# VectorE's chain of slot tables and gather rows in five parts behind five successive shared tiles

## The reference

```
x = x + attention(layernorm(x), ctx, ctx, masks)
xf = layernorm(x)
ys = geglu(xf @ Ws1 + bs1) @ Ws2 + bs2            # shared expert, 512 hidden
logits = (xf @ Wr + br) / 1.5                     # 12 experts
top_val, top_idx = top_k(logits, 2);  w = softmax(top_val)
yE[e] = geglu(xf @ We1[e] + be1[e]) @ We2[e] + be2[e]   # 768 hidden
x = x + ys + sum over the two chosen experts of w * yE
```

## Time and profile before

| | us |
|---|---|
| median of 3 runs | 753.22 |
| lowest, highest | 750.91, 760.72 |
| profiled execution, its own time | 759.51 |
| its span in the profile | 757.7 |
| PE busy in it | 646.5 (85%) |
| VectorE busy | 484.7 (64%) |
| POOL busy | 347.5 (46%) |
| ScalarE busy | 300.7 (40%) |

### The profile page before, as it was taken

The page is one execution under the profiler, slowest core; times in us unless marked ns, Lnnn a source line. Parts: engine busy times, 40 slices in busy tenths (PEclk is TensorE's granted clock), DMA queues, the critical chain, the costliest instruction groups (busy, mean ns, idle before and its releaser), DMA issues.

```text
span 757.7 us, 14868 instructions
## 1 busy us (share of the span) xinstructions
PE 646.5 (85%) x4276; PEld 536.5 (71%) x4277; DVE 484.7 (64%) x1077; ACT 300.7 (40%) x685; POOL 347.5 (46%) x404
## 2 busy tenths in 40 slices
PE   7889989998968287699999999999999999993264
PEld 6778777877755265587878878787887878883163
DVE  7667767768734237976666767676666666762086
ACT  4445555554532042135434444444444444430021
POOL 3950000000120707796497489478974860027500
PEclk9989999999965668999999999999999999996687
DMA  9964522536010300553443544353545320113311
GB/s 294 402 218 163 210 107 101 208 140 251 24 47 1 117 8 17 177 181 114 153 166 119 193 148 167 123 193 133 194 129 177 121 78 28 35 42 119 90 42 56
DMA packets 48178, 100.07 MB, mean 132 GB/s; under 512 B 4624, under 2 KB 23824, under 8 KB 48144
## 3 DMA queue, kind: packets, MB, share of 16 engines
q1 hardware_dynamic: 36320, 51.06, 19.0%
q0 software_dynamic: 11120, 48.24, 19.0%
q10 hardware_dynamic: 704, 0.33, 0.2%
HBM read 58.19 MB, written 39.19 MB: 129 GB/s over the span
## 4 chain that ended last, share of the span: by engine, by line
PE 72%; DVE 10%; issue 7%; another core or an unknown queue 5%; ACT 5%; POOL 1%; DMA 1%; DVEq 0%; ACTq 0%; SPq 0%; POOLq 0%
PE ps_s L657 27%; PE ps_o L704 8%; PE ps_o L708 5%; PE ps_t L557 4%; PE ps_o L569 4%; PE ps_s L545 4%; PE ps_t L671 3%; PE ps_t L484 2%; ACT probT L832 2%; PE ps_x L484 2%; PE ps_s L540 2%; DVE x_all L1403 2%; PE ps_x L679 1%; PE ps_s L671 1%
## 5 line engine op out<-in xcount | busy, mean ns | idle before, releaser
L657 PE MATMUL ps_s<-ring,xTh 128*128 (+1 forms) x644 | 193.0, 422 | 13.2 <-issue 12.6
L657 PEld LDWEIGHTS ps_s<-ring,xTh 128*128 128x128 f32 x644 | 112.1, 192 | 31.4 <-issue 13.5
L1313 DVE TENSOR_TENSOR ag<-ps_s,up_bias 128x512 f32<-128x512 f32 x145 | 99.9, 689 | 26.3 <-remote 14.4
L657 PE MATMUL ps_s<-ring,xTl 128*128 (+1 forms) x322 | 101.6, 397 | 0.0
L1437 POOL TENSOR_TENSOR ring<-stage,ring 128x512 fp32r<-128x512 f32 x80 | 100.6, 1291 | 1.2
L1425 POOL TENSOR_TENSOR ve<-mv,eps 128x2 f32<-128x2 f32 x16 | 3.9, 247 | 207.2 <-DVE mv L1122 166.0
L704 PE MATMUL ps_o<-ring,hTh 128*128 x258 | 95.9, 409 | 1.0 <-DVE hTl L1322 1.0
L708 PE MATMUL ps_o<-ring,hTl 128*128 (+1 forms) x322 | 92.5, 287 | 0.0
L906 ACT ACTIVATE hTh<-ps_t 128x256 fp32r<-128x256 f32 x118 | 45.2, 384 | 109.8 <-PE ps_t L671 80.1
L899 ACT ACTIVATE ps_s<-ag 128x256 f32<-128x256 f32 x161 | 62.6, 389 | 48.8 <-DVE ag L1313 45.2
L1318 DVE TENSOR_TENSOR ag<-ag,ps_s 128x256 f32<-128x256 f32 x161 | 67.7, 421 | 20.2 <-ACT ps_s L899 2.1
(11 more groups left out here) (253 smaller groups left out, 1275.1 us busy)
## 6 DMA issues: line engine op xcount, KB each, us to landing
rows_in<-y_row SPq DMA_DIRECT2D x8, 3328.0 KB, 11.2
stage<-in_w POOLq DMA_DIRECT2D x12, 1536.0 KB, 6.7
stage<-in_w POOLq DMA_DIRECT2D x12, 768.0 KB
up_bias<-in_bias POOLq DMA_DIRECT2D x12, 768.0 KB, 4.6
xrow<-rows_in SPq DMA_DIRECT2D x43, 128.0 KB, 2.3
rows_out<-y_row SPq DMA_DIRECT2D x43, 128.0 KB, 1.7
cbuf<-in_ctx SPq DMA_DIRECT2D x8, 256.0 KB, 3.2
xn_all<-xn2p SPq DMA_DIRECT2D x8, 256.0 KB
```

The lines of the kernel that those rows point to most:

```text
L657: last = pe_.matmul(ps_s[:, i, :], x[:, c, :], weights(place, off + c * full + i * 2 * D, 2 * D), start=n == 0, stop=n == 5)
L1313: vec.tensor_tensor(ag[i][:, :, :].rearrange("p a n -> p (a n)"), ps_s[:, i, :], bias, ALU.add)\
```

## The change

The two functions of the chain are cut into five pieces: slot_experts, slot_places, slot_rows, out_rows_base with out_rows(0), and out_rows(1). The first stays behind tile 3, the others stand behind tiles 4, 5, 6 and 7. The two operations that write tab_ring and tab_need move into the second piece. The loop over tiles 4 to 7 on VectorE is written out. No other engine's stream changes; the waits of SyncE, POOL and PE are where they were.

```diff
--- before.py
+++ after.py
@@ -1239,22 +1239,23 @@
             def over_tiles(a):
                 return a.rearrange("p (o e) -> p o e", o=1).broadcast_to(wide)
 
-            def out_rows():
-
-                shape = [P, TILES, E]
+            def out_rows_base():
+
                 chain(vec.tensor_tensor(base_e[:, :], cum_e[:, :], tiles_e[:, :], ALU.subtract))
                 chain(vec.scalar_tensor_tensor(base_e[:, :], base_e[:, :], float(P), const[:, C_REGION:C_REGION + E],
                                                ALU.mult, ALU.subtract))
                 chain(vec.tensor_tensor(pos[:, :, :], pos[:, :, :],
-                                        base_e[:, :].rearrange("p (o e) -> p o e", o=1).broadcast_to(shape), ALU.add))
-                for k, pick in enumerate((pick1, pick2)):
-                    chain(vec.tensor_tensor(eq[:, :, :], pos[:, :, :], pick[:, :, :], ALU.mult))
-                    chain(vec.tensor_reduce(best[:, :], eq[:, :, :], AX.X, ALU.add))
-                    last = vec.tensor_copy(idx_out[:, k, :], best[:, :])
-                    if k == 0:
-                        chain(last)
-                    else:
-                        last.then_inc(out_rows_ready, 1)
+                                        base_e[:, :].rearrange("p (o e) -> p o e", o=1).broadcast_to([P, TILES, E]), ALU.add))
+
+            def out_rows(k):
+
+                chain(vec.tensor_tensor(eq[:, :, :], pos[:, :, :], (pick1, pick2)[k][:, :, :], ALU.mult))
+                chain(vec.tensor_reduce(best[:, :], eq[:, :, :], AX.X, ALU.add))
+                last = vec.tensor_copy(idx_out[:, k, :], best[:, :])
+                if k == 0:
+                    chain(last)
+                else:
+                    last.then_inc(out_rows_ready, 1)
 
             def first_rows():
 
@@ -1268,15 +1269,23 @@
                 chain(vec.tensor_scalar(tiles_e[:, :], cnt_s[:, :], 1.0, None, ALU.max))
                 chain(vec.tensor_tensor_scan(cum_e[:, :], ones_e[:, :], tiles_e[:, :], 0.0, ALU.mult, ALU.add))
 
-            def tile_tables():
+            def slot_experts():
 
                 vec.tensor_scalar(tab_cum[:, :], cum_e[:, :], float(FRONT), None, ALU.add)
                 chain(vec.tensor_tensor(past[:, :, :],
                                         const[:, C_SLOT:C_SLOT + SLOTS].rearrange("p (s o) -> p s o", o=1).broadcast_to(wide),
                                         over_tiles(cum_e[:, 0:E - 1]), ALU.is_ge))
                 chain(vec.tensor_reduce(slot_e[:, :], past[:, :, :], AX.X, ALU.add))
+
+            def slot_places():
+
                 chain(vec.tensor_tensor(past2[:, :, :], past[:, :, :], over_tiles(const[:, C_STEP:C_STEP + E - 1]), ALU.mult))
                 chain(vec.tensor_reduce(slot_r[:, :], past2[:, :, :], AX.X, ALU.add))
+                vec.tensor_copy(tab_ring[:, :], slot_r[:, :])
+                vec.tensor_scalar(tab_need[:, :], slot_e[:, :], 2.0, None, ALU.add)
+
+            def slot_rows():
+
                 chain(vec.tensor_tensor(past2[:, :, :], past[:, :, :], over_tiles(tiles_e[:, 0:E - 1]), ALU.mult))
                 chain(vec.tensor_reduce(slot_f[:, :], past2[:, :, :], AX.X, ALU.add))
                 chain(vec.scalar_tensor_tensor(slot_f[:, :], slot_f[:, :], -1.0, const[:, C_SLOT:C_SLOT + SLOTS],
@@ -1284,8 +1293,6 @@
                 chain(vec.scalar_tensor_tensor(slot_f[:, :], slot_e[:, :], float(REGION // P), slot_f[:, :],
                                                ALU.mult, ALU.add))
                 vec.tensor_scalar(tab_row[:, :], slot_f[:, :], float(P), None, ALU.mult)
-                vec.tensor_copy(tab_ring[:, :], slot_r[:, :])
-                vec.tensor_scalar(tab_need[:, :], slot_e[:, :], 2.0, None, ALU.add)
                 vec.tensor_scalar(sel_ind[:, :], slot_e[0:P, :], const[0:P, C_ROW:C_ROW + 1], None,
                                   ALU.is_equal).then_inc(tables_ready, 1)
 
@@ -1379,10 +1386,17 @@
                 tile(s, s, False, False)
             first_rows()
             tile(ROUTED_IN + 1, ROUTED_IN + 1, False, False)
-            tile_tables()
-            out_rows()
-            with ve.Fori(ROUTED_IN + 2, FRONT) as s:
-                tile(s, s, False, False)
+            slot_experts()
+            assert FRONT == ROUTED_IN + 6
+            tile(ROUTED_IN + 2, ROUTED_IN + 2, False, False)
+            slot_places()
+            tile(ROUTED_IN + 3, ROUTED_IN + 3, False, False)
+            slot_rows()
+            tile(ROUTED_IN + 4, ROUTED_IN + 4, False, False)
+            out_rows_base()
+            out_rows(0)
+            tile(ROUTED_IN + 5, ROUTED_IN + 5, False, False)
+            out_rows(1)
             ve.wait_ge(tables_ready, 1)
             tile(FRONT, 0, True, False, prev_s=FRONT - 1)
             choice_weights()
```

## The result

The changed kernel takes 768.55 us (median of 6 runs, 765.14 to 770.88) against 756.34 for the kernel before (6 runs, 750.35 to 760.72): a ratio of 1.016 with a 95% interval of 1.0095 to 1.0226, some 12 us slower. The forecast was 759.4 us in a range of 754 to 766: a loss of 6.2 us over a median of 753.22. All ratios here are taken over the fast runs of each kernel (those within 1.5% of its fastest), so they can differ from the quotient of the medians by up to 0.004. The profiled execution took 768.98 us, its span is 767.0; before, 759.51 and 757.7.

What follows compares the result with a forecast made beforehand. PE was taken as the bound (72% of the span). Tile 8 starting 4.0 us later, the cover's gain included, plus 1.7 for clock and 0.5 for choice weights gave 6.2 over 753.22: 759.4 us, range 754 to 766.

Steps and rivals of the forecast that it cites:

- The hole: Before tile 8: PE idle 8.9 us waiting for expert 0's bias rows, so tile 8 starts 4.0 us later than before.
- a landing of 4.8: Before tile 8: the bias rows' transfer takes 4.8 us from POOL's issue, bounds 4.4 and 7.6.
- the table reads 1.75: Before tile 8: PE's sequencer reads two tables after the landing, 1.75 us uncovered, bounds 1.0 and 1.75.
- Rivals A: Before tile 8: bias rows don't hold PE, so the 4.88 us gain stands alone, 748.3 us; chance 10%.
- C: Routed stage: expert 1's weights come late, beyond a margin of some 14 us; 764.4 with 5 us over; chance 4%.
- the cover of the parts: Tiles 4 to 7: the split chain hides largely behind PE, each part free up to 1.25 us; gain 4.88 us.
- the model of the loop through VectorE (3.76 + d): Shared tiles: a tile takes 3.76 us plus its part d through VectorE, against 5.01 for PE alone.
- mark to x_all 0.45: Shared tiles: VectorE's x_all starts 0.45 us after the tile's mark, its last down-product matmul.
- clock: Tile 8, after the idle time: a stretch at half clock costs PE 1.7 us, lower bound nothing.
- choice weights: Behind tile 8: three small VectorE operations meet POOL's shifted conversions, 0.5 us more, between none and 2.3.
- the anchor: Whole kernel: the forecast adds its loss to 753.22 us, the median of the runs before.
- Rival B: Tiles 4 to 7: cover fails, parts lie in full on PE's path, 5.2 us more, 764.6; chance 8%.

Runs made afterwards that it cites:

- e3: Changed kernel, chain's buffers moved to unused memory, POOL not waiting for the chain before bias rows and conversions: 759.81 us, ratio 1.006 to before, long chip.
- e7: Changed kernel, buffers moved so bias rows load early, POOL waiting for the chain's end before converting expert 1's weights: 691.91 us, ratio 0.9915 to before, short chip.
- e11: Same kernel as e7, on a long chip: 756.59 us, ratio 1.0014 to the kernel before.
- e15: Kernel before with only the chain's last three operations, out_rows(1), moved from behind tile 3 to behind tile 7: ratio 1.0191, long chip.
- e10: Changed kernel without the last 8 scatters of rows, long chip: ratio 1.0054 to the kernel before.
- e1: Kernel before, unedited, profiled once more on a long chip: 755.28 us.
- e9: Changed kernel, unedited, run again on a long chip: 771.04 us, ratio 1.0194 to the kernel before.
- e2: Changed kernel, unedited, run again on a long chip: ratio 1.0111 to the kernel before.
- e13: Changed kernel, unedited, run again on a long chip: ratio 1.0117 to the kernel before.
- e16: As e3, but the chain cut into finer parts, the last two behind the second and third routed tiles: ratio 1.001 to before, long chip.
- e4: Changed kernel with 30 filler matmuls before PE's wait for the bias rows, long chip: ratio 1.0116 to the kernel before.
- e6: Kernel before without the last 8 scatters of rows, short chip: ratio 0.9984 to the kernel before.
- e12: Kernel before, unedited, profiled again on another long chip: 753.14 us.

## Why the prediction was right or wrong

**Right: the mechanism and the large term.** The hole was forecast at 8.9 us and measured at 8.65: POOL's issue 0.61 behind the chain's end (idx_out ends at 340.53 + 0.17 = 340.70, the issue starts at 341.31), a landing of 4.8 (4.65), the table reads 1.75 (1.77). That the bias rows cause it is shown by e3, e7 and e11, which have no hole, and by e15, which has only it. Rivals A (no hole) and C (expert 1 late) are out; for C, mark 9 to the end took 401.6 us against 402.4 before. The transfer supports the row against the estimate of the Trainium skill (DMA: Bandwidth & Descriptors, Anatomy of one DMA), 3.8 us: 4.65 here.

**Wrong in size: the cover of the parts, 4.88 forecast, 2.95 measured.** By tiles, the forecast was 6.27, 5.31, 5.86, 5.54, and the profile has 5.51, 8.31, 5.70, 5.39. Three tiles came out better than forecast, so the model of the loop through VectorE (3.76 + d) was sound; with no late signal the four tiles took 5.06, 5.17, 5.70, 5.41 (e10). Tile 5 alone lost 3.0. The step that failed is "mark to x_all 0.45", taken from the earlier trace rows as if it held everywhere; behind mark 4 it was 3.47. In the kernel before, the lump covered the time in which POOL issues its last scatters; the parts expose it. Without late signals the cover is worth 6.4 us (27.74 less 21.33 on the short chip), more than forecast. 1.2 of that is tile 4: the forecast let PE reach its down product at 317.61, a time read from a stretch in which the clock happened to be at half, in the kernel before:

```profile
312.00:314.00 2.00, 2.00 (x12) 1.90 (x11) 1.56 (x6) 0.59 (x2) 1.51 (x2) 0.55 0.91 342
314.00:316.00 2.00, 2.00 (x9) 1.52 (x7) 1.90 (x4) 0.18 (x1) 1.39 (x3) 0.60 0.25 88
```

In e1 and e10 the clock is 1.00 over the four microseconds behind mark 3. The same stretch gave the 0.45 from mark to x_all, which is 0.33 at full clock.

**Wrong in size: clock and choice weights, 2.2 forecast, 3.2 measured in the first pair and 3.5 as the mean of four profiles.** The stretch at half clock was taken as long as the two in the earlier trace rows, 2.9 and 4.3 us, of which the first follows 5.07 us of idle time. After 8.65 us of idle time it was about 6 us of work in the first pair and in e9, and tile 8 lost 2.8 where 1.7 was forecast. In e2 and e13 it was about 3 us and tile 8 lost 1.5 and 1.3, but the clock fell again in tile 9. What decides between the two lengths isn't shown. The choice weights were bounded well: 0.93 instead of 0.17 for the last, 1.0 us more for the three in the first pair (0.7 to 1.6 in the four profiles), of which tile 9 shows 0.4 there. That is between nothing and the 1.9 by the rule of the Trainium skill (SBUF — State Buffer, Who interferes with whom). The 1.9 counted three operations; the reciprocal among them has one input and kept its 0.25. e3 and e16 agree with this rule in kind: operations with two inputs in SBUF and tensor_scalars stretched to between 1.1 and 1.7 us where they met POOL's conversions, though not each did (sel_ind took 0.23 in e3 and 1.30 in e16), and the reductions never.

These two, with 0.3 less for the hole, put the sum at 8.75 instead of 6.2.

**Wrong: the anchor and the width.** 753.22 was the median of three runs, on which I put an uncertainty of 2 us. Three more runs moved it to 756.34. With the terms as measured, 753.22 + 8.75 = 762.0 was inside the range. The result lies 6.6 above that: 3.1 are the anchor, 3.5 what the first pair's medians differ by beyond the 8.75 in its marks. The step that failed is "so a median may lie 2 us off". By their ratios the four pairs of the two kernels differ by 12.1, 8.4, 14.7 and 8.8 us, 11.0 on average; tiles 4 to 9 explain 9.0. The 2 us between are no more than the intervals allow, and no run shows where they lie.

**Rival B** (PE idle before each down product, because the cover fails for every part) is out: the marks show three of the four tiles as covered as forecast, and the fourth failed by another mechanism.

## What to carry to other kernels

Before you spread a chain over a loop, list who waits for its last operation; a few short operations moved late can cost more than the lump they leave (e15). Here the split needed the memory freed that the waiting load shares with it: with that it gained on the short chip (0.9915, e7) and nothing that a measurement tells on a long one (e11). A lump may also cover other things, such as stretches in which another engine's transfers make signals late, and exposes them when it goes. When three runs spread by 10 us, put that spread into the range, and look in several profiles for the stretch that scatters. Price a hole by the distance between the marks around it, not by its own length: 5.07 and 6.25 us of idle time stood in stretches of the same 12.7.

## What the hardware showed that I had not expected

**Late signals beside indirect transfers.** On the long chips, engines that wait for PE start up to 3.5 us after the start of PE's record (0.28 us long), while or shortly after POOL issues a run of indirect transfers. (3.5 is the longest for x_all in tiles 4 to 9.) Removing the last 8 of them removed the late signal of tile 5 (e10), which is one profile against four, and where they end earlier against mark 4 the signal is less late (e4, e16). Longer ones stand in the attention, in both kernels alike: ScalarE's outT in the kernel before waits 7.39 and 11.47 us, "remote", with POOL's runs of 8 and 16 scatters beside it (205.2 to 215.3 and 245.4 to 265.6); that these have the same cause is argued, not shown. The longest of all in that profile, 15.49 us, is ScalarE's xTh at 711.20, within the run of the final gathers (675.74 to 715.80 us), which are indirect transfers too. Not every signal inside such a run is late: the earlier trace rows begins with one that isn't. What delays them I don't know.

```profile
216.90 0.60 ACT L837 ACTIVATE outT<-ps_o 128x512 f32<-128x512 f32 x1 [7.39 <-remote]
...
265.52 0.60 ACT L837 ACTIVATE outT<-ps_o 128x512 f32<-128x512 f32 x1 [11.47 <-remote]
```

**Chips differ.** The same kernel takes 697 us on one chip and 755 to 756 on three, and the short one shows no late signals at all. Of these roughly 60 us, 25 lie ahead of mark 3 and 34 behind mark 9 (284.4 and 367.4 us in e6, against 309.1 and 401.9 in e1), where the other scatters and the final gathers are; whether late signals make up all of it wasn't tried. The mean granted clock differs as well, 0.967 in e6 against 0.915 in e1 and 0.925 in e12; whether that is a cause or follows from the longer idle times isn't shown.
